# A paged attention kernel: one weight chunk a period on GpSimd, cache copies issued by SyncE in four and eight parts

## The reference

```python
x = x + einsum('bsi,boi->bso', x, weight[adapter_ids])
q, k, v = x @ Wq.T, x @ Wk.T, x @ Wv.T            # 32, 8, 8 heads of 128
q, k = rope(rmsnorm(q, q_norm_w)), rope(rmsnorm(k, k_norm_w))
k_all = concat([k_cache[block_table], k]); v_all = concat([v_cache[block_table], v])  # 512 + 128 keys
probs = softmax(mask(q @ k_all.T / sqrt(128)))
x = x + (probs @ v_all) @ Wo.T
```

## Time and profile before

| what | value |
| --- | --- |
| median of the runs | 1092.32 us (1089.48 to 1095.16, 2 runs) |
| profiled execution | 1094.0 us, span of the core 1092.0 us |
| PE busy | 977.4 us (90%) |
| DVE busy | 920.3 us (84%) |
| ACT busy | 796.4 us (73%) |
| POOL busy | 863.5 us (79%) |
| bytes moved by DMA | 173.69 MB, mean 159 GB/s |
| mean granted clock of TensorE | 0.97 |

### The profile page before, as it was taken

The page is one execution under the profiler, slowest core; times in us unless marked ns, Lnnn a source line. Parts: engine busy times, 40 slices in busy tenths (PEclk is TensorE's granted clock), DMA queues, the critical chain, the costliest instruction groups (busy, mean ns, idle before and its releaser), DMA issues.

```text
span 1092.0 us, 20813 instructions
## 1 busy us (share of the span) xinstructions
PE 977.4 (90%) x5617; PEld 559.3 (51%) x5617; DVE 920.3 (84%) x1942; ACT 796.4 (73%) x2202; POOL 863.5 (79%) x1184
## 2 busy tenths in 40 slices
PE   6787997789868999989998999899998999899997
PEld 4344554455434555545554555455555555455554
DVE  6576876578868999989997999979997999899994
ACT  4364655468677888878887888878887888777873
POOL 3656567558858998889898998889888988989881
PEclk9889999899999999999999999999999999999999
DMA  8688977738897777766778677876776777757862
GB/s 256 174 230 239 246 229 221 207 106 160 179 187 137 142 154 157 138 136 142 158 140 162 128 144 157 148 145 140 154 139 139 153 158 140 130 99 133 152 140 64
DMA packets 505733, 173.69 MB, mean 159 GB/s; under 512 B 429121, under 2 KB 487762, under 8 KB 505618
## 3 DMA queue, kind: packets, MB, share of 16 engines
q1 hardware_dynamic: 482752, 149.76, 65.5%
q10 hardware_dynamic: 21714, 20.25, 6.1%
q0 software_dynamic: 1152, 2.36, 0.8%
HBM read 98.11 MB, written 31.86 MB: 119 GB/s over the span
## 4 chain that ended last, share of the span: by engine, by line
PE 42%; DVE 19%; issue 4%; POOL 2%; ACT 2%; DVEq 0%; POOLq 0%; ACTq 0%
PE S L1729 10%; DVE pr L1359 5%; DVE pr L1331 5%; DVE sm L1344 4%; PE Y L1655 4%; PE Y L1657 4%; PE Y L1656 4%; PE Q L1656 3%; PE Q L1655 3%; PE Q L1657 3%; PE O L1655 2%; PE O L1656 2%; PE O L1657 2%; PE T L1661 2%; POOL wl L644 2%
## 5 line engine op out<-in xcount | busy, mean ns | idle before, releaser
L1359 DVE SCALAR_TENSOR_TENSOR pr<-pr,rc,upper 128x640 f16<-128x640 f32 x220 | 235.2, 1069 | 20.5 <-ACT upper L1025 13.8
L1331 DVE CUSTOM_DVE_ANT_0 pr<-S,mask,rst 128x640 f32<-128x640 f32 x256 | 224.4, 876 | 30.8 <-PE S L1729 19.2
L1025 ACT ACTIVATE upper<-pr,rc 128x640 f16<-128x640 f32 x220 | 170.3, 820 | 75.7 <-DVE rc L1347 75.6
L1045 ACT ACTIVATE pr<-pr,nb 128x640 f32<-128x640 f32 x256 | 209.6, 819 | 17.5 <-DVE nb L1331 14.5
L1729 PE MATMUL S<-kh,qh 128*128 128x320 f16 x512 | 113.0, 303 | 41.9 <-DVE nb L1331 41.9
L754 POOL TENSOR_TENSOR m<-m 128x512 f32<-128x512 f32 x63 | 81.7, 1297 | 78.1 <-DVE m L1403 78.1
L1729 PE MATMUL S<-kl,qh 128*128 128x320 f16 x512 | 112.3, 301 | 0.9 <-POOL kl L644 0.9
L1729 PE MATMUL S<-kh,ql 128*128 128x320 f16 x512 | 112.5, 302 | 0.0
L644 POOL TENSOR_TENSOR wl<-wraw,wh 128x512 f16<-128x512 f32 x71 | 104.2, 1468 | 5.9
L1729 PEld LDWEIGHTS S<-kh,qh 128*128 128x128 f16 x512 | 45.9, 99 | 116.1 <-DVE nb L1331 71.1
L1655 PE MATMUL Q<-wh,xh 128*128 128x512 f16 x256 | 99.9, 390 | 4.1 <-issue 2.8
(11 more groups left out here) (218 smaller groups left out, 2719.4 us busy)
## 6 DMA issues: line engine op xcount, KB each, us to landing
wraw<-in_wall SPq DMA_DIRECT2D x74, 256.0 KB, 3.5
cache_rows<-in_kv ACTq DMA_DIRECT2D x80, 224.0 KB
rawk<-cache_rows SPq DMA_DIRECT2D x55, 256.0 KB
vraw<-cache_rows SPq DMA_DIRECT2D x55, 256.0 KB, 4.6
cache_rows<-in_kv SPq DMA_DIRECT2D x36, 224.0 KB
second<-in_lw SPq DMA_DIRECT2D x4, 1024.0 KB
first<-in_lw SPq DMA_DIRECT2D x3, 1024.0 KB
cache_rows<-in_kv SPq DMA_DIRECT2D x16, 192.0 KB, 3.6
```

Of the source, the lines that this page charges most:

```text
L1025: e.activation(upper16[:, g, :], pr[:, slot(u, g), :], ACT.Copy, scale=rc[:, u % 2, g:g + 1]).then_inc(a_f1, 1)
L1045: e.activation(pr[:, slot(u, g), :], pr[:, slot(u, g), :], ACT.Exp, bias=nb[:, u % 2, g:g + 1], scale=-1.0, accum_out=sm[:, u % 2, g:g + 1 ...
L1331: e.tensor_tensor_reduce(pr[:, slot(u, g), :].rearrange("p (a n) -> p a n", a=2), S[:, :, 0:320], mask[:, u % NB, :].rearrange("p (a n) -> ...
L1359: e.scalar_tensor_tensor(out=lower16(u, g), in0=pr[:, slot(u, g), :], scalar=rc[:, u % 2, g:g + 1], in1=upper16[:, g, :], op0=ALU.mult, op ...
```

## The change

It does five things. (1) The weight tables move: GpSimd makes one chunk in every period of a head's eight, and VectorE makes chunks 5 (period -2) and 9 (period 1), directly behind `largest(i, 0)`. ScalarE's high part stands one period ahead of it. Q chunks are loaded two periods earlier, each as soon as its own predecessor was split. (2) `score_scales` goes from GpSimd to ScalarE (`a_rst`); the query weight's scale is folded into `koff`, and the two `var` operations become one. (3) All cache copies are issued by SyncE, 16 DMAs in each of periods 0 to 7; a copy is written as 8 parts by 14 rows of 512 elements for sequences 0 to 3 and as 4 parts by 16 rows of 1024 elements for sequences 4 to 7. (4) `NL = 4`: units 4 to 7 load K and V from the copy. `load_k` now stands behind the period's copies. (5) GpSimd splits the values of units 0 to 7 too, and in the prologue the first keys are split by ScalarE and VectorE.

```diff
-NL = NB + 1
+NL = 4
-COPY_SP = (0, 1, 1, 1, 1, 1, 1, 2, 0, 1, 1, 1, 2, 0)
-COPY_ACT = (2, 2, 3, 2, 2, 3, 3, 2, 1, 0, 0, 0, 0, 0)
...
-          0: (-6, 0), 1: (-5, 0), 2: (-4, 0), 3: (-3, 0), 4: (-2, 0), 5: (-2, 1),
-          6: (-1, 0), 7: (0, 0), 8: (0, 1), 9: (1, 0)}
-LO_DVE = {(0, 6): (1, 1), (0, 7): (1, 1), (0, 9): (1, 1)}
...
+          0: -7, 1: -6, 2: -5, 3: -4, 4: -3, 5: -3, 6: -2, 7: -1, 8: 0, 9: 0}
+LO_DVE = {(0, 6): 1, (0, 8): 1, 5: -2, 9: 1}
+LO_POOL = {(0, 7): 1, (0, 9): 1, (1, 0): -4, (1, 1): -4, (1, 2): -3, (1, 3): -3, (1, 4): -2,
+           (1, 5): -2, 0: -6, 1: -5, 2: -4, 3: -3, 4: -2, 6: -1, 7: 0, 8: 1}
+LOAD_AT = {(1, 0): -8, (1, 1): -8, (1, 2): -7, (1, 3): -7, (1, 4): -7, (1, 5): -6,
+           0: -12, 1: -11, 2: -11, 3: -10, 4: -9, 5: -8, 6: -6, 7: -6, 8: -5, 9: -5}
...
+def copies_of(period):
+    return [((period + NL) % NB, t) for t in range(NGRP)] if 0 <= period < NB else []
...
         def copy_page(e, b, k, number):
-            rows = slice(2 if b >= NL - NB else 4, 2 * NK)
-            e.dma_start(copy[rows, b, k, :].rearrange("r (s n) -> s r n", s=16),
-                        kv[rows, bass.ds(number, 1), :].rearrange("r a (s n) -> (a s) r n", s=16)
+            rows, parts = (slice(2, 2 * NK), 8) if b < NL else (slice(0, 2 * NK), 4)
+            e.dma_start(copy[rows, b, k, :].rearrange("r (s n) -> s r n", s=parts),
+                        kv[rows, bass.ds(number, 1), :].rearrange("r a (s n) -> (a s) r n", s=parts)
                         ).then_inc(d_copy[b], 16)
...
             def load_w(hk, c):
-                if hk >= 1:
+                if hk >= 1 and c < 4:
+                    e.wait_ge(w_lo[0], parts_made(hk - 2, 0) + c + 1)
+                elif hk >= 1:
                     e.wait_ge(w_lo[group(c)], parts_made(hk - 1, group(c)))
...
             for i in range(0, NA):
+                if i + 3 < NB:
+                    load_x(i + 3)
+                if NL <= i + 1:
+                    load_v(i + 1)
                 if 2 <= i + 1 < NB:
                     load_mask(i + 1)
                 next_weights(i)
                 if i + 3 < NL:
-                    for t in range(NT):
+                    for t in range(2, NT):
                         load_kt(e, kt_regs, i + 3, t)
...
-                else:
-                    load_k(e, i + 3)
                 for b, t in copies_of(i):
                     copy_pages(b, t)
+                if i + 3 >= NL:
+                    load_k(e, i + 3)
...
+            def score_scales(j):
+                e.wait_ge(g_pow, j + 1)
+                e.wait_ge(g_kvr, j + 1)
+                if j >= 2:
+                    e.wait_ge(v_max, 4 * (j - 1))
+                e.activation(rst[:, j % 2, 0:G], pw[:, j % 2, 0:G], ACT.Copy,
+                             scale=f32(kvr[:, j % 2, 1:2])).then_inc(a_rst, 1)
```

More of the change, by code:

```diff
@@ L99, in at_period @@
         for c in range(NWC):
[L100 to L104, removed]
+            general = c in table and hk > 0 and not (hk == 1 and c < 6)
+            at = table.get((hk, c), table[c] if general else None)
+            if at is not None and NB * hk + at == period:
                 found.append((hk, c))
     return found
[L109 to L116, removed]
+def copies_of(period):
+    return [((period + NL) % NB, t) for t in range(NGRP)] if 0 <= period < NB else []
 def build(nc, x, xt, lw, wall, kv, ids_lens, table, pages, qkw, consts, iota, out):
@@ L259, in hi_made @@
             first_c, size = ((0, 4), (4, 2), (6, 4))[g]
-            return size * hk + c - first_c + 1
+            return size * hk + c - first_c + 1 - (1 if g == 1 and hk else 0)
         def parts_made(hk, g):
@@ L358, in build @@
         id_reg = nc.sync.alloc_register("id")
-        copy_regs = [nc.scalar.alloc_register(f"copied{j}") for j in range(12)]
+        copy_regs = [nc.scalar.alloc_register(f"copied{j}") for j in range(4)]
         def bc(src, n):
@@ L569, in _ @@
             e.dma_start(kwc[:, :], qkw[D:2 * D].unsqueeze(1)).then_inc(d_kwc, 16)
-            for t in range(2):
+            for t in range(3):
                 load_kt(e, kt_regs, 0, t)
@@ L649, in _, with split_w @@
             w_scaled = [0]
-            def split_w(period, place):
-                for hk, c in at_period(LO_POOL, period, place):
+            def split_w(period):
+                for hk, c in at_period(LO_POOL, period):
                     e.wait_ge(w_hi[group(c)], hi_made(hk, c))
@@ L938, in split_chunk, with split_w @@
                              scale=w_scale(hk, group(c))).then_inc(w_hi[group(c)], 1)
-            def split_w(period, place):
-                for hk, c in at_period(HI_ACT, period, place):
+            def split_w(period):
+                for hk, c in at_period(HI_ACT, period):
                     split_chunk(hk, c)
@@ L1006, in v_squares, with first_keys_hi @@
                 square(v_left[:, u % 2, :], vraw[:, u % 3, :], kvss[:, u % 2, 0:1]).then_inc(a_kvss, 1)
-            def copied_pages(period):
-                pages_of = []
-                for n, (b, t) in enumerate(copies_of(period, act=True)):
-                    first_page = NPG * b + 4 * t
-                    regs = copy_regs[4 * n:4 * n + 4]
-                    e.load(regs, page[0:1, first_page:first_page + 4])
-                    numbers = [e.snap(r, min_val=0, max_val=63) for r in regs]
-                    pages_of += [(b, 4 * t + j, numbers[j]) for j in range(4)]
-                return pages_of
+            def first_keys_hi():
+                e.wait_ge(g_kvs, 1)
+                e.activation(kh[:, 0, 0:512], raw_k(0), ACT.Copy, scale=k_scale(0)
+                             ).then_inc(made_kh, 1)
+            def score_scales(j):
[5 more added lines that the diff above has]
+                             scale=f32(kvr[:, j % 2, 1:2])).then_inc(a_rst, 1)
             def upper_plane(u, g):
@@ L1071, in _ @@
             split_chunk(0, 4)
-            split_chunk(0, 5)
+            w_square(0, 1)
             l0_hi(0)
-            for c in range(1, 4):
+            for c in range(2, 4):
                 w_square(0, c)
-            key_squares(0)
             for c in range(4):
                 split_chunk(0, c)
+            key_squares(0)
             k_squares(0)
@@ L1114, in _ @@
                     exp(i, 1)
+                    for t in range(2):
+                        load_kt(e, copy_regs, 3, t)
                 q_squares(j)
```

272 lines of the change are left out of this document (120 added, 152 removed), and 10 rows, old and new, of tables (HI_ACT, LO_POOL, SQUARES).

## The result

The changed kernel takes 1182.64 us (median; 1182.60 to 1182.69, 2 runs) against 1092.32: a ratio of 1.083, 95% interval 1.071 to 1.095. It is slower. The profiled execution has a span of 1180.8 us, 88.8 over that of before (1092.0).

The account below looks back on a forecast made before the run. Bound taken: a loop from rope products through GpSimd's list, `sm` and `largest` to scores, plus head's-end waits. 1094 + 115 (copies) - 52 (later gains) = 1157, forecast 1156 us from the median; own range 1125 to 1200, overall 1016 to 1190.

Parts of the forecast that it names:

- The confined copies: Periods 0 to 8: copies use only four or eight engines, 43.7 or 19.1 us a sequence, so K lands late: +115 us.
- Periods 5 to 8: Starts at 257, 289, 321 and 344 us, after waits for K behind copies and for weight loads; period 9 at 366.
- the relief of 4.4 and 2.75 us: Periods 0 to 8: ScalarE's copy issues and the `rst` wait go, leaving 14.6 us from K's squares to the next period.
- The steady period: Plain periods: GpSimd's shorter list closes the 0.49 us gap before the second scores; 13.8 us a period, 14.4 if nothing closes.
- The loop through `sm`: Steady period: rope products, GpSimd's list from `m` to `wl`, `sm`, `largest`, scores; `sm` can lose 0.9 us of excess.
- What is late next is TensorE itself: Steady period: with the gap closed, TensorE's own products set the time, 13.6 us at best; 13.8 taken.
- The 0.85 us: GpSimd between `m` and `wl`'s end loses `rst` (0.36), one `var` (0.27) and a 0.22 us wait, so `wl` ends earlier.
- The head's end: Periods 22 and 23: 0.5 us of wait left, 0.8 for VectorE's chunks, 1.3 for unit scales; 2.6 us a head.
- Sixteen engines for every copy: Rival, copies in periods 0 to 8: all sixteen engines take them, about 203 us for 214; 1031 us (1005 to 1066), chance 0.34.
- Half confined: Rival, copies: engines take turns or four run nearly twice as fast, 22 us a sequence; 1092 us (1070 to 1120), chance 0.08.
- The third, on the missing steady gain: Rival: `sm` waits for GpSimd's next operation, periods stay 14.4, some 26 of 52 us lost; 1182 with confined copies, chance 0.08.
- The sign in the earlier trace: Small DMA `iot`, 8 rows, has no landing time and `il`, 128 rows, has 2.8 us: a weak sign of confinement.

Follow-up runs that it names:

- e1: Changed kernel with every copy written as 16 parts outermost, still all issued by SyncE in the same places: 1075.0 us.
- e4: Changed kernel with copies in 8 parts outermost for all sequences, also 4 to 7: 1110.5 us.
- e10: Changed kernel, copies still in 4 and 8 parts, with K ahead of the period's copies, head 2's two weight loads a period later, `var` as two operations: 1138.6 us.
- e7: Changed kernel with copies in 16 parts and GpSimd's one `var` operation written as two again: 1057.3 us.
- e12: Kernel before the change with GpSimd's two `var` operations written as one of 128x5: 1096.5 us.
- e11: Changed kernel with 16-part copies, K ahead of copies, head 2's two weight loads later, `var` in two, and chunk 5 split by GpSimd, not VectorE: 1058.2 us.
- e3: Kernel before the change with its copies written as 4 parts, its last four (repeated) copy DMAs left out: 1193.1 us.

## Why the prediction came out as it did

The forecast was slower, 1156 us, by copies confined to four and eight engines. The sign and the cause hold, and `e1` to `e4` and `e10` show them from both sides. The range of 1016 to 1190 says little by itself, as it holds both signs; what bears the forecast out is the cause. The time is some 26 us over the forecast: 12 us in the start of period 9 and 14 in what follows it.

- **The confined copies.** K of units 4, 5 and 6 was to land at 141, 192 and 242 us and was squared at 142.75, 192.49 and 243.10. The mechanism was right, but the closeness is luck. At the 112 GB/s of the idle stretch a sequence takes 37.5 us, not 43.7, and the rest of a round, which I put at 7 us, is longer by nearly as much: rounds of 50.7 forecast, 49.7 and 50.6 measured. And the first copy was issued at 51.10 us, not at 43, which the quicker copies made up for.
- **Periods 5 to 8**, forecast to start at 257, 289, 321 and 344 and period 9 at 366, started at 262, 297, 328, 353 and 377. The two stalls of SyncE at the weight loads are there as described: they were to end at 252 and 284 and ended at 253.2 and 288.2. Two sizes were too small. A round of copies on eight engines takes 23.5 to 24.0 us from its first issue to the squares of K (254.58 to 278.11 for the first), where 22 were put, four times over. And the way from K's squares to the next period's start, put at 14.6, is 18.9 us ahead of period 5 and 15.9 ahead of period 9: the relief of 4.4 and 2.75 us that was taken off the 21.7 of before came only in part. Together the start of period 9 is 11 us late; the 12th in the table is the 1 us of the prologue, which was counted apart.
- **The steady period** was forecast at 13.8 us. It is 14.38 (mean of the first seven of a head, units 16 to 55), where it was 14.42: nothing was gained. The loop through `sm` was read rightly: the late `sm` of a period, over 1 us long in all 40 of these periods before, takes 0.15 to 0.17 us in 24 of them now (0.17 at 564.01), and the wait for `nb` is all but gone. What I missed is what comes earlier when GpSimd's list gets shorter: `kh` meets VectorE's plane operation, and the wait for `kmin` takes the place of that for `nb`. "What is late next is TensorE itself" is the step that failed, worth 10 us in units 16 to 55 and 3.5 in the last periods, by `e7`. Even there the seven take 14.10 and not 13.8; that its head of 113.4 us is near the 113.0 forecast is owed to the head's end, which costs less than was put.
- **The 0.85 us** that GpSimd was to gain is for a third (`var`, 0.27 us) worth nothing: `e12` shows that it is absorbed in `kh`.
- **The head's end** was forecast at 2.6 us over eight plain periods; it is 0.3 (115.3 less 8 x 14.38). Its last period fell from 18.7 to 14.7 us, and that is nearly the whole gain of the steady part. The wait is 0.91 us, not 0.5, but the clock stays up, as said, and the 1.3 us that I kept for the clock and the unit scales aren't there. The chunk on VectorE is 0.6 us (`e11`), nearer the 0.75 of its duration than the half of it.
- **The tail**: the last period and what follows gained 3.1 us, which I hadn't looked for.
- **The rivals.** Sixteen engines for every copy: no. `e1` is the kernel that this rival described, and its price was too low as well: 1075.0 us against 1031 (1005 to 1066), mostly for the 237.3 us of periods 0 to 8, where 203 were put. Half confined: no. The third, on the missing steady gain, had a chance of 0.08 and gave 1182, the time measured. Its condition came true, periods of 14.4 outside the head's end, though by `kmin` and not by `sm`. Its number is luck in part: the head's end gave back half of the 26 us that it lost, and the copies cost 12 more.
- **The sign in the earlier trace rows**, an issue without a landing time, is too weak to use: in `e1` the copies of 14 rows in 16 parts show one (4.3 us) and those of the kernel before, of the same shape, don't.

As the Trainium skill has it (DMA: Bandwidth & Descriptors, Why a DMA increments its semaphore by 16 and not by 1), the count of engines is the largest up to 16 that divides the slowest dimension of both sides, and the lowest-numbered ones are taken. The share of 0.28 to 0.30 in stretches of copies of four parts, where four of sixteen engines would be 0.25 and other DMAs add to it, agrees with the count. `e3`'s late page loads fit a backlog on engines that all DMAs share; which engines they are no view here shows.

## What to carry to other kernels

In a copy from DRAM to DRAM, read the outermost count of both sides as the number of DMA engines before anything else is costed, and keep it at 16 (343 us for periods 0 to 8 with 4 and 8, 237 with 16). When all engines wait for a DMA, look at the DMA share in that very window: 0.30 said here that the transfer was narrow, 1.04 that the engines were full. Put what is needed soon ahead of bulk copies in an issuer's list, and nothing that waits in front of either (25 and 20 us here). And before crediting an engine off the critical path with earlier work, look at which operation of its neighbour the shifted one will meet.

## What was unexpected of the hardware

One more small operation on GpSimd took 13.5 us off periods 16 to 62, by a shift of 0.15 us against VectorE. A GpSimd cast of 128x512 takes 0.62 us when it starts within 0.01 us of a VectorE operation with two tensor inputs, and that one then takes 1.30 us in place of 0.88; when it starts 0.15 us behind, it takes 1.20 itself and VectorE's keeps its 0.88. The layouts with 16 parts and with the rows outermost, with pieces of 1 and 16 KB, differ by 9 us in single runs, so the size of a piece matters little here beside the count.
